# Output biases of the experts in a table of their own, read through a register, and weight loads released by the down multiplication

## What is computed

```python
# layer 0: 4096 tokens, 8 experts, top 2       (D = 128, H = 512)
for e in range(8):
    h = gelu(flat @ W1[e] + b1[e])
    out = out + combine[:, e:e + 1] * (h @ W2[e] + b2[e])
# layer 1: 4096 tokens, 4 experts, top 2
for e in range(4):
    h = gelu(xi @ We1[e] + be1[e])
    yo = h @ We2[e] + be2[e]
    out = out + yo * combine_w[..., e:e + 1]
```

## Time and profile before

| | us |
|---|---|
| median of 3 executions | 840.44 |
| lowest and highest | 838.6, 843.49 |
| the profiled execution | 837.16 |
| its span, first to last instruction | 835.4 |
| PE busy | 711.1 |
| DVE busy | 553.1 |
| ACT busy | 484.6 |
| POOL busy | 452.4 |

### The profile page before, as it was taken

How to read it: one execution, slowest core, us unless ns; L and a number is a source line. 1 busy time by engine, 2 the same in 40 slices (tenths; PEclk the granted TensorE clock), 3 DMA queues, 4 the chain that set the end, 5 groups by cost and what they waited for, 6 DMA issues and landing times. The chain is left out here.

```text
span 835.4 us, 17043 instructions
## 1 busy us (share of the span) xinstructions
PE 711.1 (85%) x5311; PEld 487.3 (58%) x5311; DVE 553.1 (66%) x1306; ACT 484.6 (58%) x917; POOL 452.4 (54%) x397
## 2 busy tenths in 40 slices
PE   3968888899898999889999888999979488999880
PEld 3742223333333333379898687898858377988770
DVE  7999999988888888433333478367356474543354
ACT  4864677788787888745455365786601144444340
POOL 6933456889898887645454444100054652554451
PEclk9997999999999999799999999999866579999995
DMA  7973522223222221357877965600012311777846
GB/s 227 287 222 115 175 92 68 87 74 91 73 86 95 74 92 50 109 158 220 270 233 243 297 205 182 184 1 2 1 39 81 123 38 54 218 232 225 276 131 191
DMA packets 96461, 117.44 MB, mean 141 GB/s; under 512 B 10552, under 2 KB 72296, under 8 KB 96408
## 3 DMA queue, kind: packets, MB, share of 16 engines
q1 hardware_dynamic: 88376, 100.22, 39.5%
q0 software_dynamic: 8032, 16.58, 5.7%
HBM read 82.30 MB, written 34.32 MB: 140 GB/s over the span
## 5 line engine op out<-in xcount | busy, mean ns | idle before, releaser
L750 POOL DMA_INDIRECT yg_dram<-work x135 | 134.5, 997 | 157.8 <-DVE work L1931 114.8
L1344 ACT ACTIVATE work<-wide,work 128x256 f32<-128x256 f32 (+1 forms) x324 | 129.5, 469 | 129.8 <-PE wide L970 124.3
L1496 DVE TENSOR_REDUCE work<-wide 128x4 bf16<-128x1024 f32 x128 | 155.7, 1226 | 19.3 <-PE wide L847 11.9
L981 PE MATMUL wide<-work 128*128 128x128 f32 x1272 | 154.9, 275 | 0.0
L981 PEld LDWEIGHTS wide<-work 128*128 128x128 f32 x1272 | 149.0, 192 | 0.8
L970 PE MATMUL wide<-xT,work 128*128 128x256 f32 (+1 forms) x552 | 130.1, 378 | 12.9 <-issue 8.4
L970 PEld LDWEIGHTS wide<-xT,work 128*128 128x128 f32 x552 | 98.0, 190 | 27.5 <-issue 13.8
L711 POOL TENSOR_TENSOR work<-work,biasT 128x1024 f32<-128x1024 f32 x32 | 75.7, 2366 | 42.2 <-ACT work L1282 41.6
L711 POOL TENSOR_TENSOR yy<-yy,biasT 128x1024 f32<-128x1024 f32 x32 | 75.7, 2366 | 30.3 <-ACT yy L1282 29.9
L1289 ACT ACTIVATE yy<-yy 128x1024 f32<-128x1024 f32 x64 | 67.4, 1055 | 25.7 <-DVE yy L1802 25.7
L841 PE MATMUL wide<-biasA,turnb 128*128 128x512 bf16 x256 | 79.4, 393 | 3.0 <-DVE work L1496 2.6
(11 more groups left out here) (315 smaller groups left out, 1205.9 us busy)
## 6 DMA issues: line engine op xcount, KB each, us to landing
work<-in_wcat SPq DMA_DIRECT2D x73, 578.0 KB
xg_dram<-empty SPq DMA_DIRECT2D x35, 260.0 KB, 2.8
work<-xg_dram SPq DMA_DIRECT2D x66, 130.0 KB
stk_dram<-yy SPq DMA_DIRECT2D x16, 384.0 KB, 3.6
work<-stk_dram SPq DMA_DIRECT2D x64, 96.0 KB
work<-stk_dram SPq DMA_DIRECT2D x64, 64.0 KB
yy<-yg_dram SPq DMA_DIRECT2D x8, 512.0 KB, 6.5
biasT<-ext_dram SPq DMA_DIRECT2D x8, 384.0 KB
```

Source lines behind the costliest of these rows:

```text
L750: g.indirect_dma_start(out=yg_dram[l], out_offset=bass.IndirectOffsetOnAxis(ap=yid[v][:, s_:s_ + 1].bitcast(u32), axis=0), in_=yb[u][:, s_ ...
L981: last = mm(YP[u][:, s_ * D:(s_ + 1) * D], hb[u][:, c, s_ * P:(s_ + 1) * P], wb[v][:, HID + c * D:HID + (c + 1) * D], start=(c == 0), stop ...
L1344: A(hb[u][:, c, 0:n * P], bank[2 + 2 * u + c // 2][:, (c % 2) * TS:(c % 2) * TS + n * P], ACT.Gelu, bias=wb[v][:, bc:bc + 1]).then_inc(m[" ...
L1496: V.tensor_reduce(nmax[:, :, 2 * place(t):2 * place(t) + 2].rearrange("p c e -> p e c"), into[:, :].rearrange("p (e c k) -> p e c k", e=2, ...
```

## The change

Three things change together.

1. The output biases of all experts of a layer are loaded once, as a table `b2_bc` of 8 (or 4) times 128 numbers on each partition. In layer 0 SP issues this load (512 KB) after the last rows of attention are done, ahead of the weights of tiles 2 and 3. In layer 1 it is 256 KB, behind the weights of expert 3. DVE waits for the table ahead of `copy_rows(2)`, and in each `keep_dense`.
2. `outputs(j)` reads `widx` into a register of DVE, and adds the bias from `b2_bc` at that column. Since an expert's row 128·e is also its column, the same number serves.
3. A weight load takes 1028 columns instead of 1156 (514 KB instead of 578 KB), and from tile 4 on it is released by `down` of tile j-4 instead of by `yb` of tile j-4.

```diff
@@ load_weights, SP
-                        sp.wait_ge(m["yb"], j + (1 - NWB))
-                    sp.dma_start(wb[v], wcat[bass.ds(row, P), :]).then_inc(m[f"W{v}"], 16)
+                        sp.wait_ge(m["down"], j + (DENSE[l] + 3 - NWB))
+                    sp.dma_start(wb[v][:, 0:WROW - D], wcat[bass.ds(row, P), 0:WROW - D]).then_inc(m[f"W{v}"], 16)
@@ SP
+                def load_biases():
+                    ne = (E0, E1)[l]
+                    sp.dma_start(b2_bc[:, 0:ne * D].rearrange("p (e d) -> p e d", d=D),
+                                 wcat.rearrange("(e p) w -> p e w", p=P)[:, :, WROW - D:WROW]).then_inc(s_b2, 16)
...
                     sp.wait_ge(A0["s"], NB + 1)
+                    load_biases()
                     load_weights(2, 2)
                     load_weights(3, 3)
...
-                        sp.dma_start(wb[e], wcat1[e * P:(e + 1) * P, :]).then_inc(moe[1][f"W{e}"], 16)
+                        sp.dma_start(wb[e][:, 0:WROW - D], wcat1[e * P:(e + 1) * P, 0:WROW - D]).then_inc(moe[1][f"W{e}"], 16)
+                    sp.dma_start(b2_bc[:, 0:E1 * D].rearrange("p (e d) -> p e d", d=D),
+                                 wcat1.rearrange("(e p) w -> p e w", p=P)[:, :, WROW - D:WROW]).then_inc(s_b2, 16)
@@ outputs, DVE
+                    c = place_of(j) if l else j
+                    at = widx[0:1, c:c + 1] if isinstance(c, int) else widx[0:1, bass.ds(c, 1)]
+                    first = dve.value_load(at, min_val=0, max_val=((E0, E1)[l] - 1) * D)
                     dve.wait_ge(m["down"], j + (DENSE[l] + 3))
...
-                                    mid(wb[v][:, WROW - D:WROW], n), ALU.add).then_inc(m["yb"], 1)
+                                    mid(b2_bc[:, bass.ds(first, D)], n), ALU.add).then_inc(m["yb"], 1)
...
                 dve.wait_ge(m["y"], DENSE[l] + 4)
+                dve.wait_ge(rou[l]["routed"], 1)
+                dve.wait_ge(s_b2, 16 * l + 16)
@@ keep_dense, DVE
                 dve.wait_ge(moe[1]["down"], j + 3)
+                dve.wait_ge(s_b2, 32)
...
-                                mid(wb[j % NWB][:, WROW - D:WROW], 2), ALU.add).then_inc(moe[1]["y"], 1)
+                                mid(b2_bc[:, j % NWB * D:j % NWB * D + D], 2), ALU.add).then_inc(moe[1]["y"], 1)
```

More of the change, by code:

```diff
@@ L317, in build @@
         yw = [take(2) for _ in range(NWB)]
+        b2_bc = take(E0 * D)
         xTd = [biasA[:, :, :].rearrange("p h b -> p (h b)").bitcast(fp32)[:, b * S:(b + 1) * S] for b in range(NB // 2)]
@@ L391, in build @@
         com = [phase_sems("combine", 0, COM + ["stats", "normed"]), phase_sems("combine", 1, COM + ["dense"])]
-        s_out = sem("out_stored")
+        s_out, s_b2 = sem("out_stored"), sem("output_biases_loaded")
         A0 = phase_sems("attend", 0, ["init", "stk00", "stk01", "stk10", "stk11", "v_sb", "A", "Ared", "mT", "nmT", "M0", "M1", "B", "Sv", "Sa", "Sp", "E", "PV", "oTs",
```

## The result

The changed kernel took 857.14 us in the median of 6 runs (851.94 to 860.52), against 840.67 for the kernel before beside it: a ratio of 1.0176, 95% interval 1.0142 to 1.021. On another chip the same pair gave 1.0134 (1.0075 to 1.0193). It is slower, by 1.3 to 1.8%, and not by the 0.2% of the forecast; 857.14 lies above the range of 836 to 848.

The account below looks back on a forecast made before the run. PE is busy 711.1 of 835.4 us; in layer 0 a two-tile ring of stores, DVE and POOL slows it. Terms +3.4 - 2.7 - 0.3 + 1.2 + 0.1 = +1.7 us on 840.44 gave 842.1 us, range 836 to 848.

Parts of the forecast that it names:

- The ring of two tiles: Layer 0 tiles: store lands, DVE adds and multiplies, POOL issues, next store lands; 8.1 us a turn where PE needs 7.5.
- the read's term: DVE's register read in outputs, exposed only right after a wait for a store: 7.5 x 0.45 = +3.4 us.
- The price: One read on DVE, taken from SP's reads of widx: 0.27 us load plus 0.15 register work, with small steps 0.45 us.
- The count: Exposed reads: 6.5 turns from 13 tiles of layer 0, plus one before the up at 478.58, 7.5 in all.
- The cover by the sequencer's lead: Where DVE works without a pause, its sequencer is 1.06 us ahead, so a 0.45 us read fits in unseen.
- rival 1: DVE's sequencer can't read SBUF while older operations run, or the read costs 0.7 us: 846.7 us, chance 0.22.
- Smaller loads: Weight loads 64 KB smaller: landings 0.41 us earlier in 6.5 turns, -2.7 us, and -0.3 us near the end of layer 1.
- The release by down: Weight loads released by down instead of the bias addition: gain put at nothing, with 2 us at most.
- The tables: Bias table loads: layer 0's delays up(2), +1.2 us (ends 0 and 3); layer 1's delays down(3) of the dense tiles, +0.1.
- Rival 2: Data traffic binds the layer 0 stretch, so smaller loads bring back all 6.0 us: 835.8 us, chance 0.18.
- The second sign: Late in layer 0, the up at 483.91 would not come later against its neighbours.
- The first sign: Late in layer 0, the up at 478.58 would come 0.4 us later against its neighbours.

Follow-up runs that it names:

- the early read: Changed kernel with the register read moved ahead of DVE's wait for the stores, behind the xT copy: 804.89 against 803.1 us for the kernel before, ratio 1.001.
- the pair on one chip: Two kernels differing in load size and where the bias is read: kernel before plus tables, 1.003; changed kernel without read, loads released by yb, 0.9982.
- the pair on two: Changed kernel without the register read, on two chips: weight loads of 1156 columns, 1.0057 of the kernel before; loads of 1028 columns, 0.9985.
- the pair with the early read: Changed kernel with the read ahead of DVE's store wait: weight loads released by yb, 1.0056 of the kernel before; released by down, 1.001.

## Why the prediction was wrong

**What bounds the kernel** held. The ring of two tiles sets the pace of the tiles of layer 0, and time between a landing and the next store comes out at PE: in the turn shown, 0.84 us more there (1.94 against 1.10) and 1.07 us more for the turn.

**The step that failed is the read's term**, 7.5 x 0.45 = +3.4 us, where the read alone cost 9.8. It has three parts, and each was too small.

- *The price*, 0.45 us. It was read from SP, as load and register work. The rows of the read on DVE's sequencer, and of the address at the addition (ns min/median/max):

```profile
L1933 DVEq FUSED_REGOPS  x89: 46/190/210, 366.2 to 825.4; - x89
L1933 DVEq TENSOR_LOAD <-widx x69: 299/306/555, 365.6 to 825.0; - x69
L1933 DVEq SEQ_ASSERT  x69: 23/23/35, 366.4 to 825.6; - x69
```

```profile
L1940 DVEq FUSED_REGOPS  x69: 57/57/64, 367.2 to 827.7; - x69
```

306 + 190 + 23 + 57 = 576 ns, and small steps between them. The load and its register work took 306 and 190 ns here, against the 270 and 152 on SP that the forecast took over, and the assertion and the address were left out of it. How much of it shows can be read where DVE comes out of a wait. A written-out tile, in after and then in the kernel before:

```profile
483.57 0.16 DVE L1913 COPY work<-work 128x2 f32<-128x2 f32 x1
...
484.31 0.42 DVE L1940 TENSOR_TENSOR work<-wide,work 128x256 f32<-128x256 f32 x1 [0.58 <-issue]
```

```profile
475.65 0.16 DVE L1904 COPY work<-work 128x2 f32<-128x2 f32 x1
475.72 0.42 DVE L1928 TENSOR_TENSOR work<-wide,work 128x256 f32<-128x256 f32 x1
```

From start to start 0.74 us instead of 0.07, so 0.67 are exposed. In the loop, where the column of `widx` comes out of a register as well, it is 0.98 us in the turn above (446.68 to 447.66). Before, in the turn of the earlier trace rows, it was 0.14:

```profile
448.83 0.16 DVE L1904 COPY work<-work 128x2 f32<-128x2 f32 x1
448.97 0.42 DVE L1928 TENSOR_TENSOR work<-wide,work 128x256 f32<-128x256 f32 x1
```

So 0.84 us are exposed there, and the early read shows the other side: from the small operation to the addition it is 0.29 us with only the address between. The Trainium skill ("DMA: Bandwidth & Descriptors", Latency and other measured facts) has about 600 ns as the floor of such a load. For the load's own row the trace disagrees, 306 ns here and 270 on SP; for the whole group of instructions, 576 ns, it is near. By that figure the forecast's sum would have been +4.2, and still far too small.

- *The count*, 7.5. It was worked out as turns, with one read in each, the other covered. The row "L1940 <- issue" counts 31, in both layers. Of the kernel after in 388:476 alone:

```profile
DVE work L1940 <- issue: 11.2, 16, 1.1
```

16 where the prediction had 6.5; the second profile has 17. The second tile of a turn is worked off right behind the first, after the end of the same wait, and pays as well: 0.83 and 0.74 us of idle time in the turn above. That the sequencer hasn't got its lead back by then is how I read it; no run isolates it. And of the 9 places in layer 1 (5.7 us between 700 and 830) the prediction had none. A right price times a right count would still not be the time: the read alone made DVE stand 15.6 us, and the kernel 9.8 us longer.

- *The way to PE*. The prediction sent the read's time to PE by the ring alone. The `xT` copy of the next tile stands behind the addition in DVE's order, and PE's up waits for it: 1.10 us ahead of 449.27.

In the stretch from up(8) to up(29) the read cost 90.6 - 82.3 = 8.3 us (5.2 in the second profile of after), and alone 94.5 - 84.4 = 10.1, where the prediction had 6.5 x 0.45 = 2.9. These are single profiles.

**The cover by the sequencer's lead** held where the prediction saw it. Behind the batch statistics:

```profile
485.11 1.64 DVE L1482 BATCH_NORM_STATS2 stats<-yy 128x6 f32<-128x128 f32 x8
...
486.67 0.41 DVE L1906 COPY xT<-wide 128x256 f32<-128x256 f32 x1
486.99 0.15 DVE L1912 TENSOR_TENSOR work<-work,spare 128x2 int32<-128x2 f32 x1
487.06 0.16 DVE L1913 COPY work<-work 128x2 f32<-128x2 f32 x1
487.13 0.41 DVE L1940 TENSOR_TENSOR work<-wide,work 128x256 f32<-128x256 f32 x1
```

```profile
L1933 DVEq TENSOR_LOAD <-widx x1: 309/309/309, 485.0 to 485.0; - x1
```

The read for the addition at 487.13 ran at 485.0, just ahead of the statistics, while the multiplication L1943 (484.77, 0.42 us) was under way. So rival 1's mechanism, a sequencer that can't read SBUF while older operations are under way, is refuted, while its price of 0.7 us was near. Its 846.7 us was too low as well.

**Smaller loads**: -3.0 forecast, some 4 us by the pair on one chip and 6 by the pair on two. With their intervals, both agree with the forecast; where in the kernel the time comes back is less sure. In the stretch the forecast had -2.7 us. The kernels without a read took 82.3 and 83.8 us there with small loads, and 84.3 to 85.3 with full ones, which leaves 0.5 to 3.0.

**The release by down** was put at nothing: 0.9982 against 0.9985, and 1.0121 against 1.0134. Right as far as these pairs tell; each is across two chips, and the pair with the early read leaves 0.5% open.

**The tables**: +1.3 forecast. From the last addition of attention to up(2) it was 4.89 us before (361.34 to 366.23); in the kernel after:

```profile
361.52 3.27 PE L979 MATMUL wide<-xT,work 128*128 128x256 f32 x8 [0.52 <-DVE bufA L1828]
...
367.33 1.99 PE L979 MATMUL wide<-xT,work 128*128 128x256 f32 x8
```

The last addition of attention began at 361.04, so it is 6.29 us, 1.4 later; 1.2 had been forecast. But PE hardly waited there: its up(1) took 3.27 us instead of 1.99, at a granted clock of 0.71 (361.5 to 367.3), and its last instruction before up(2) ended at 367.20. So this profile can't tell the table from the clock. The kernel with release by yb and no read can. Its up(1) took 1.99 us, and its up(2) stood 1.87 us for the weights, against 0.41 before, and came 6.35 us after the addition: 1.46 us later. Both tables alone cost 1.003, 2.5 us, with 1.3 inside the interval. For layer 1's table, put at +0.1, no run isolates a price.

**Rival 2**, that the data bind, is refuted as a whole: the stretch slowed down while the DMA share fell to 0.75. It had the direction of the small loads right.

**The signs.** The up at 478.58 was to come 0.4 us later against its neighbours, and that at 483.91 not. Before, the steps from up(29) to up(30) to up(31) were 5.44 and 5.33 us (473.14, 478.58, 483.91). In after they are 6.73 and 5.45 (480.45, 487.18, 492.63), in the second profile 4.80 and 5.33. The second sign held in both. In the first profile 6.73 also holds a fall of the clock: PE stood idle 2.76 us ahead of 487.18, that up took 2.58 us, and the granted clock was 0.84 and 0.82 from 485 to 490 and from 490 to 495 us. The first sign can be read from the landing just ahead of it (475.57 before, 483.49 and 479.13 after): 3.01 us from there to the up before, 3.69 and 3.68 after. That is 0.7 later, where 0.4 had been forecast. DVE's waits for stores in 388:476 became fewer:

```profile
DVE work L1912 <- DMA yg_dram<-work: 23.3, 9, 3.8
...
DVE work L1912 <- issue: 9.2, 3, 3.1
```

Twelve and 32.5 us with the three long ones that have no releaser, instead of 18 and 35.9. Tiles 8 to 29 were to take 84 us again, and took 90.6 and 87.5.

**The sum put right.** Read +1.26% (measured alone), all the rest -0.15%, together +1.1%, or 9 us: 850 instead of 842.1. The two measurements of after are 852.23 and 857.14. What of the difference is interplay, what is the clock and what is scatter stays open. The kernels with the early read and small loads stay at 1.001 to 1.0056. The stalls that the early read still makes in the second tile of a turn are one reason that the traces show; what they cost was not measured apart. No kernel of this study is measurably faster than the one before.

## What to carry to other kernels

A register read on a compute engine is paid where that engine has just come out of a wait, and it costs its range check and its address as well as its load (0.67 to 0.84 us here, not 0.3). So put it ahead of the wait that it would follow, where most of its price goes (alone it cost 1.3% behind the wait and 0.1% ahead of it), and take the count from the places at which the engine resumes, in every tile that is worked off in the same burst. When work is added to an in-order engine, follow every consumer of what stands behind it: here PE waited for a copy that had nothing to do with the read. And look at the granted clock of each stage before two profiles are compared: in the kernel after one long idle time of PE came with a lower clock, and with two reads 5.2 us of a stretch's loss were busy time.

## What the runs showed of the hardware

**A small VectorE operation held for a whole POOL addition.** At the start of layer 0, the kernel with the table ahead of the row loads (L1919 and L1920 are the two small operations, L1912 the `xT` copy):

```profile
353.63 8.59 POOL L675 TENSOR_TENSOR bufC<-bufC,shb_bc 128x1024 f32<-128x1024 f32 x4
354.22 0.42 DVE L1912 COPY xT<-wide 128x256 f32<-128x256 f32 x1 [1.27 <-PE wide L1002]
354.56 1.28 DVE L1919 TENSOR_TENSOR work<-work,spare 128x2 int32<-128x2 f32 x1
355.76 2.22 DVE L1920 COPY work<-work 128x2 f32<-128x2 f32 x1
357.90 0.41 DVE L1912 COPY xT<-wide 128x256 f32<-128x256 f32 x1
358.23 1.88 DVE L1919 TENSOR_TENSOR work<-work,spare 128x2 int32<-128x2 f32 x1
360.03 2.21 DVE L1920 COPY work<-work 128x2 f32<-128x2 f32 x1
```

POOL's four additions take 8.59 / 4 = 2.15 us each, so they end at 355.78, 357.93, 360.07 and 362.22. DVE's operations on 2 columns, 0.15 us elsewhere, end at 355.84, 357.98, 360.11 and 362.24: each just behind a POOL addition, and as long as what was left of it. The copies out of PSUM between them keep their 0.42 us. Not every operation of this kind is held. In the kernel before, at the same place, L1903 took 0.40 and 1.81 us and ended within 0.05 us of a POOL addition's end, but its copies L1904 took 0.15 us. With POOL held until those operations were through:

```profile
352.40 0.15 DVE L1920 TENSOR_TENSOR work<-work,spare 128x2 int32<-128x2 f32 x1
352.47 0.16 DVE L1921 COPY work<-work 128x2 f32<-128x2 f32 x1
...
353.18 4.32 POOL L675 TENSOR_TENSOR bufC<-bufC,shb_bc 128x1024 f32<-128x1024 f32 x2 [1.48 <-DVE work L1921]
```

The Trainium skill ("SBUF — State Buffer", SBUF: two separate sides) states that the two engines share a pair of ports as an exclusive lock, held for a whole instruction, which an operation of VectorE needs in a 2-port mode, or with two SBUF inputs beside an operation of POOL that reads SBUF, and that the loser is fully blocked. The trace agrees for L1919, which has two SBUF inputs: 0.15 us became 1.28 and 1.88, and went back to 0.15. For the copy L1920, with one input, the trace doesn't show in which mode it ran, so why it was held here and not in the kernel before stays open.

**The same read on two sequencers.** A load of one number into a register took 306 ns on DVE's sequencer in the median, 299 at least and 555 at most, against 270 on SP's with 12 and 813 as ends, and did not wait for DVE's data path.
